# Perceiver block on one core: logits one block sooner, a Sinkhorn chain's lead of 12, and tile 2 mixed by TensorE

## What is computed

```
x_norm = x * rsqrt(mean(x * x) + eps)
H_res_logits = (x_norm @ W_res.T).reshape(B, T, 4, 4) + H_res_base     # pre and post likewise, 4 each
step, 50 times:  u = -logsumexp(Z + v, axis=-1);  v = -logsumexp(Z + u, axis=-2)      # Z = logits / 0.1
H_res = exp(Z + u + v);  H_res = (1 - g) * I + g * H_res
x_pre = einsum('btnc,btn->btc', x_streams, softmax(H_pre_logits));  y = x_pre @ W_branch
out = x + einsum('btij,btjc->btic', H_res, x_streams) + einsum('btc,btn->btnc', y, softmax(H_post_logits))
```

## Time and profile before

| | |
|---|---|
| median of 3 runs | 1117.78 us (1116.27, 1117.78, 1118.06) |
| the profiled execution | 1117.16 us |
| its span | 1115.4 us |
| granted TensorE clock, mean | 0.986 |
| busy: TensorE, VectorE, ScalarE, GpSimd | 95%, 73%, 43%, 17% |
| chain that ended last, by engine | TensorE 88%, VectorE 9%, DMA 1%, ScalarE 1% |

### The profile page before, as it was taken

The page is one execution under the profiler, slowest core; times in us unless marked ns, Lnnn a source line. Parts: engine busy times, 40 slices in busy tenths (PEclk is TensorE's granted clock), DMA queues, the critical chain, the costliest instruction groups (busy, mean ns, idle before and its releaser), DMA issues.

```text
span 1115.4 us, 17534 instructions
## 1 busy us (share of the span) xinstructions
PE 1057.4 (95%) x6308; PEld 888.9 (80%) x6308; DVE 816.2 (73%) x1862; ACT 475.9 (43%) x1012; POOL 190.6 (17%) x186
## 2 busy tenths in 40 slices
PE   5999999999999999999999999999999999998727
PEld 3888888788888888888888888888888878886515
DVE  6787667676667879766668877666627788837998
ACT  4553444344444446544444465423213344432315
POOL 0000000233223232333233220000001032320000
PEclk9999999999999999999999999999999999999878
DMA  9785676245543333344445312799935423000001
GB/s 240 150 204 127 153 163 156 50 109 109 113 98 86 75 76 72 70 94 97 112 95 108 76 38 52 161 217 241 210 68 104 73 42 57 3 14 1 1 1 76
DMA packets 184540, 111.26 MB, mean 100 GB/s; under 512 B 108040, under 2 KB 174344, under 8 KB 184480
## 3 DMA queue, kind: packets, MB, share of 16 engines
q1 hardware_dynamic: 182224, 109.37, 45.4%
q10 hardware_dynamic: 2256, 1.11, 0.4%
HBM read 90.98 MB, written 18.94 MB: 99 GB/s over the span
## 4 chain that ended last, share of the span: by engine, by line
PE 88%; DVE 9%; DMA 1%; ACT 1%; issue 0%; ACTq 0%; POOL 0%; DVEq 0%
PE ps L606 32%; PE ps L513 15%; PE ps L573 14%; PE ps L941 9%; PE ps L499 4%; PE ps L634 4%; PE ps L617 4%; PE ps L717 1%; DVE small L2051 1%; DVE small L2055 1%; DVE small L2043 1%; DVE small L2047 1%; DVE small L2039 1%; DVE small L2035 1%; DVE xr L2185 1%; DMA raw<-in_L_xattn_q_proj_w 1%
## 5 line engine op out<-in xcount | busy, mean ns | idle before, releaser
L606 PE MATMUL ps<-wt,act 128*128 128x512 f32 x1536 | 381.0, 394 | 0.0
L606 PEld LDWEIGHTS ps<-wt,act 128*128 128x128 f32 x1536 | 278.1, 188 | 51.8 <-issue 0.4
L513 PE MATMUL ps<-wt,act 128*128 128x512 f32 x768 | 178.0, 393 | 3.9 <-DVE wt L1507 3.9
L513 PEld LDWEIGHTS ps<-wt,act 128*128 128x128 f32 x768 | 145.2, 190 | 34.6 <-DVE act L1491 4.3
L573 PE MATMUL ps<-act,wt 128*128 128x512 f32 x672 | 153.7, 390 | 0.0
L1062 ACT ACTIVATE wt<-raw 128x512 fp32r<-128x512 f32 x192 | 106.3, 625 | 94.4 <-PE ps L513 52.3
L573 PEld LDWEIGHTS ps<-act,wt 128*128 128x128 f32 x672 | 125.9, 188 | 26.0
L1499 DVE STREAM_TRANSPOSE raw<-raw 128x1024 f32<-128x1024 f32 x92 | 107.9, 1217 | 22.1 <-DMA raw<-in_L_xattn_o_proj_w 22.1
L1507 DVE TENSOR_TENSOR wt<-raw,wt 128x512 fp32r<-128x512 f32 x176 | 110.0, 683 | 17.3 <-ACT wt L1062 17.2
L941 PE MATMUL ps<-wt,act 128*128 128x512 f32 x480 | 121.3, 400 | 0.0
L2202 POOL TENSOR_TENSOR small<-small 128x4 f32<-128x4 f32 (+2 forms) x64 | 68.9, 1079 | 257.0 <-DVE small L1521 211.5
(11 more groups left out here) (162 smaller groups left out, 1226.9 us busy)
## 6 DMA issues: line engine op xcount, KB each, us to landing
xr<-in_ctx SPq DMA_DIRECT2D x64, 256.0 KB, 4.8
raw<-in_L_xattn_o_proj_w SPq DMA_DIRECT2D x32, 512.0 KB, 14.3
raw<-in_L_xattn_q_proj_w SPq DMA_DIRECT2D x28, 512.0 KB, 9.1
xr<-q_rows SPq DMA_DIRECT2D x16, 512.0 KB, 4.2
ot_hi<-spare SPq DMA_DIRECT2D x64, 128.0 KB, 2.0
act<-ot_hi SPq DMA_DIRECT2D x32, 256.0 KB, 9.6
q_rows<-G SPq DMA_DIRECT2D x28, 256.0 KB, 2.6
raw<-in_L_xattn_k_proj_w SPq DMA_DIRECT2D x8, 512.0 KB, 7.1
```

Of the source, the lines that this page charges most:

```text
L513: mm = pe.matmul(banks[t], lhs(p == 2, c, t), wt[:, n_slot, int(p == 1), c, :], start=(acc_from and q == 0), stop=(acc_to and q == 3 * NC ...
L606: mm = pe.matmul(bank, src[int(p == 2)][:, c, kt * P:(kt + 1) * P], wt[:, slot, int(p == 1), c, :], start=(q == 0), stop=(q == 3 * NC - 1))
```

## The change

It does five things. (1) The transposes and logits of tiles 0 and 1 stand earlier among TensorE's matmuls: logits of tile 0 in block 11 in place of block 12, logits of tile 1 after six matmuls of block 12 in place of after it. ScalarE's `normalise_out(0)` stands ahead of the copies for tile 1. (2) VectorE starts chain 0 ahead of the add of block 12, and runs 12 of its iterations alone, not 8. (3) TensorE mixes both halves of tile 2. Its second half goes into bank 0, which tile 0 had; an added matmul by the identity first puts `xr` into it. VectorE mixes (3, 0) and (3, 1) side by side, and no more. (4) TensorE waits ahead of tile 1's mixing until chain 1 has done all but 42 of its steps (seven iterations). (5) The store of (2, 1) stands last in SyncE's list.

The diff (`CHAIN_STEPS` is 304, the steps of a chain up to the end of its last iteration):

```diff
@@ -36,7 +36,8 @@
 ROW = 4
 NSTR, CW = 4, 256
 ITERS, EPOCH = 50, 25
-LEAD = (1, 3, 3, 1)
+LEAD = (4, 3, 3, 1, 1)
+CHAIN_STEPS = 8 + 6 * (ITERS - 1) + 2
 LAST = ((0, 0), (1, 0), (0, 1), (1, 1), (2, 0), (3, 0), (2, 1), (3, 1))
 TURNED = {(0, 0): (1, 0), (0, 1): (2, 0), (1, 0): (3, 1), (1, 1): (4, 2),
           (2, 0): (5, 3), (3, 0): (6, 5), (2, 1): (7, 4), (3, 1): (8, 7)}
@@ -160,6 +161,7 @@
         lg = [ps[:, 2, 0:24], ps[:, 4, 0:24]]
         open_banks = [(ps[:, 0, :], ps[:, 1, :]), (ps[:, 2, :], ps[:, 3, :]), (ps[:, 4, :],), (ps[:, 5, :],)]
         late_base = ps[:, 6:8, 256:512]
+        mix_banks = open_banks[0:2] + [(ps[:, 4, :], ps[:, 0, :])]
         kacc = [ps[:, 2, :], ps[:, 3, :]]
         vacc = [ps[:, 6, :], ps[:, 7, :]]
         sacc = ps[:, 4, :]
@@ -481,7 +483,7 @@
             for a, n, w in ((0, 16, w_res), (16, 4, w_pre), (20, 4, w_post)):
                 sp.dma_start(w24[a:a + n, :], w).then_inc(w24_loaded, 16)
             for t, half, signal, count in ((0, None, mix_out, 2), (1, None, mix_out, 4), (2, 0, mix_out, 5),
-                                           (2, 1, out_ready, 1), (3, 0, out_ready, 2), (3, 1, out_ready, 3)):
+                                           (3, 0, out_ready, 1), (3, 1, out_ready, 2), (2, 1, mix_out, 6)):
                 sp.wait_ge(signal, count)
                 part = slice(0, E) if half is None else slice(half * UW, (half + 1) * UW)
                 sp.dma_start(out_rows[:, t, part], xr[:, t, part]).then_inc(out_stored, 16)
@@ -922,11 +924,11 @@
 
             def mix(t):
 
-                ready = 16 * t if t < 2 else 32 + 8 * (t - 2)
-                for half, bank in enumerate(open_banks[t]):
+                for half in range(2):
+                    bank = mix_banks[t][half]
                     for i in (2 * half, 2 * half + 1):
                         for j in range(NSTR):
-                            pe.wait_ge(d_res, ready + 4 * i + j + 1)
+                            pe.wait_ge(d_res, 16 * t + 4 * i + j + 1)
                             mm = pe.matmul(bank[:, (i % 2) * CW:(i % 2 + 1) * CW], dres[t % 2][:, 4 * i + j, :],
                                            z[:, t, j * CW:(j + 1) * CW], start=False, stop=(i % 2 == 1 and j == NSTR - 1))
                     mm.then_inc(mix_done, 1)
@@ -972,6 +974,8 @@
                 def at_5():
                     if 3 <= b <= 10:
                         weigh2(b - 3)
+                    if b == 12:
+                        logits(1)
 
                 def at_11():
                     if b == 0:
@@ -979,10 +983,6 @@
                     elif b == 11:
                         turn_rows(0, 0)
                         turn_rows(0, 1)
-                    elif b == 12:
-                        logits(0)
-                        turn_rows(1, 0)
-                        turn_rows(1, 1)
                     elif b == 13:
                         turn_rows(2, 0)
                     elif b == 14:
@@ -995,6 +995,9 @@
                         turn_out2(b - 3)
                     if 1 <= b <= 8:
                         turn_query(b - 1)
+                    if b == 11:
+                        turn_rows(1, 0)
+                        logits(0)
                     if b == 15:
                         logits(2)
                         logits(3, 0, 4)
@@ -1017,15 +1020,18 @@
                     for c in range(NC):
                         mm = pe.matmul(ps[:, 3, 192:216], ones, w24T[:, c, :], start=(c == 0), stop=(c == NC - 1))
                     mm.then_inc(s24_done, 1)
-                if b == 12:
-                    logits(1)
+                    turn_rows(1, 1)
             turn_rows(3, 1)
             logits(3, 4, NC)
             for t in range(NT):
                 branch(t)
                 base(t)
-            for t in range(3):
-                mix(t)
+            mix(0)
+            pe.wait_ge(sk_step[1], CHAIN_STEPS - 42)
+            mix(1)
+            pe.wait_ge(mix_out, 1)
+            pe.matmul(mix_banks[2][1], ident[:], xr[:, 2, UW:E], start=True, stop=False)
+            mix(2)
 
 
         def ctx_dst(dst, p, kt):
@@ -1425,11 +1431,11 @@
 
             copy_rows(0, 0)
             copy_rows(0, 1)
+            normalise_out(0)
+            copy_rows(1, 0)
             sc.wait_ge(s24_done, 1)
             sc.activation(s24, ps[:, 3, 192:216], ACT.Copy).then_inc(s24_ready, 1)
-            copy_rows(1, 0)
             copy_rows(1, 1)
-            normalise_out(0)
             normalise_out(1)
             exp_chain(0)
             copy_rows(2, 0)
@@ -1449,23 +1455,23 @@
                 sc.wait_ge(h_ready, t // 2 + 1)
                 if t >= 2:
                     sc.wait_ge(mix_done, 2 * (t - 2) + 2)
-                for n in range(16 if t < 2 else 8):
+                for n in range(16):
                     sc.activation(dres[t % 2][:, n, :], ident[:], ACT.Copy, scale=hres[:, 16 * t + n:16 * t + n + 1]
                                   ).then_inc(d_res, 1)
 
             def mixed(t, half):
-                k = 2 * t + half if t < 2 else 2 + t
-                sc.wait_ge(mix_done, k + 1)
-                sc.activation(xr[:, t, half * UW:(half + 1) * UW], open_banks[t][half], ACT.Copy).then_inc(mix_out, 1)
+                sc.wait_ge(mix_done, 2 * t + half + 1)
+                sc.activation(xr[:, t, half * UW:(half + 1) * UW], mix_banks[t][half], ACT.Copy).then_inc(mix_out, 1)
 
             diagonals(0)
             diagonals(1)
             mixed(0, 0)
             mixed(0, 1)
             mixed(1, 0)
+            mixed(1, 1)
             diagonals(2)
-            mixed(1, 1)
             mixed(2, 0)
+            mixed(2, 1)
 
 
         @block.vector
@@ -2122,11 +2128,11 @@
 
             add_last(1, 1)
             logits(0)
-            add_last(2, 0)
             logits(1)
             centre_rows(0)
             centre_cols(0)
             first_iteration3(0)
+            add_last(2, 0)
             for _ in range(LEAD[0]):
                 iterate((0,))
             add_last(3, 0)
@@ -2136,8 +2142,10 @@
             for _ in range(LEAD[2]):
                 iterate((0,))
             logits(2)
+            for _ in range(LEAD[3]):
+                iterate((0,))
             add_last(3, 1)
-            for _ in range(LEAD[3]):
+            for _ in range(LEAD[4]):
                 iterate((0,))
             logits(3)
             centre_rows(1)
@@ -2187,8 +2195,7 @@
                                  out_ready if (i % 2, j) == (1, NSTR - 1) else dv)
 
             v.wait_ge(base_added, 3)
-            mix(((2, 1), (3, 0)))
-            mix(((3, 1),))
+            mix(((3, 0), (3, 1)))
 
 
         @block.gpsimd
```

## The result

| | before | changed |
|---|---|---|
| median of 20 runs | 1117.74 us | 1114.82 us |
| lowest to highest | 1116.17 to 1120.19 | 1113.61 to 1118.19 |
| the profiled execution | 1117.16 | 1116.33 |
| its span | 1115.4 | 1114.5 |

The ratio is 0.9976 (95% interval 0.9969 to 0.9982): 2.7 us faster, between 2.0 and 3.5. The medians differ by 2.9 us. Forecast were 1114.6 us, a gain of 2.9.

What follows compares the result with a forecast made beforehand. Bound: second chain's start, 50 iterations, VectorE's mixing and a store. Gains of 2.3 us (work, issue) and 0.6 (landing) make 2.9: 1114.3 from the profiled execution, 1114.9 from the median, forecast 1114.6 us; range 1113.0 to 1116.4.

Steps and rivals of the forecast that it cites:

- What bounds the kernel: End of kernel: set by the second chain's start, its 50 iterations of 1.39 us, VectorE's 24 mixing pieces and a store.
- Point 1: TensorE, blocks 11 to 12: second logits end 4.2 us sooner, at 999.9; the new order costs nothing.
- Point 2: VectorE around the last adds: twelve iterations fit with 0.2 us to spare; first chain's result comes 5.55 us sooner.
- Point 3: Mixing: starts sooner on ScalarE and TensorE, the timed wait costs 0, ScalarE's last copy ends at 1109.9.
- Point 4: VectorE's final mixing: 16 pieces, not 24, end at 1108.4; 3.7 us less, of which ScalarE leaves 2.2.
- Point 5: Last stores: the last finds the queue empty and lands in 2.1 us, not 2.7; 0.6 us gain.
- The sum: End of kernel: 2.3 us from work and issue plus 0.6 us from landing, together 2.9 us.
- rival B: VectorE before the last block's add: twelve iterations don't fit, second chain 1.4 us late, gain 1.5 us; chance 0.15.
- Rival C in its partial form: Mixing on TensorE: clock comes back 1 us later, 0.5 us of it lands on the end; likelier than full C.
- The full form: TensorE mixes tile 2 at the lower clock, 6.9 us more; kernel 4.0 us slower, about 1121; chance 0.05.

Runs made afterwards that it cites:

- front_only: Kernel before with only the new logits order and the lead of 12 iterations, old mixing kept: 1115.98 us, ratio 0.9992.
- tail_only: Changed kernel's new mixing and store order, with the kernel before's logits order, VectorE adds and lead of 8: 1120.91 us, ratio 1.0031.
- before_stores: Kernel before with SyncE's store of (2, 0) moved behind those of (2, 1) and (3, 0): 1117.32 us, ratio 0.9992.
- warm: Changed kernel plus seven unused 256-column products before tile 0, wait ahead of tile 1 at 33 steps, not 42: 1113.72 us, ratio 0.9971.
- narrow_more: Changed kernel with tile 2's eight 24-column logits products made twice in block 15, first time for nothing: 1118.25 us.

## Why the prediction was right, point by point

- *What bounds the kernel.* Right, and the two halves of the change show it: the end was VectorE's 24 pieces (`front_only` left them and gained nothing but the stores' part), and what ScalarE and TensorE do ahead of chain 1's result is free only while it fits (`tail_only`).
- *Point 1, the order at nothing.* Right. In the changed kernel the second logits end at 999.8 (999.9 forecast), with no idle time of TensorE in blocks 11 to 14.
- *Point 2, twelve iterations fit.* Right, with 0.56 us to spare (0.2 worked out) where the clock didn't fall, and chain 1 starts 5.4 us behind the last six matmuls with eight iterations or with twelve. Chain 0's result stands 5.5 us further ahead.
- *Point 3, ScalarE and TensorE.* Tiles 0 and 1: 16.2 us (16.1). First matmul of tile 2: 0.84 us behind the result (0.7). Last copy ended 8.65 us behind it (8.4). The wait cost nothing, as worked out.
- *Point 4.* 16 pieces in 6.80 us; VectorE ended 1.85 us ahead of ScalarE.
- *Point 5, the stores.* Landing 2.0 us (2.1), and `before_stores` shows the crowding by itself. Here the row of the trace was followed and not the figure of the Trainium skill, and the row was right.
- *The sum.* 2.8 us in the tail of the two traces, 2.7 (2.0 to 3.5) in the times, 2.9 forecast. The terms behind it are a little off and cancel: the end of the work gained 1.9 us (2.2 forecast), the issue and the landing 0.8 (0.7 forecast), and 0.1 lies behind the landing. In the other traces that mix tile 2 by TensorE with the lead and a cold start, the tail is 10.7 to 11.5 us, a gain of 2.3 to 3.2 over the one trace of before. That the medians agree with the forecast this closely is in part luck.
- *What the median also holds.* Among executions with a clock above 0.983, the median of the changed kernel is 1114.44 (15 executions), that of the kernel before 1116.71 (36, beside the groups): 2.3 us. Among the others it is 1116.53 (5) against 1118.14 (44): 1.6 us. The medians of all differ by more, since the changed kernel had fewer falls, 5 of 20 against 44 of 80. Whether the change does that or chance did is open; nothing in the prediction asks for it.
- *Slips in the working.* The sum gives 1114.3 from the profiled execution and 1114.9 from the median; the forecast of 1114.6 is the middle, and the metric is the median. The range doesn't follow from its own terms: 1116.3 less 3.5 and 1118.1 less 1.3 are 1112.8 and 1116.8, not 1113.0 and 1116.4. The clock came back 4.1 us after the mixing began, not 3.9. None of this moves the result out of the range.
- *What was missing.* The text named a late start of chain 1 as the sign of rival B. The sign came, and B was not the cause: the last adds waited for TensorE at the half clock. A sign that only says "late" doesn't tell who was late; the idle time before the add does (1.58 us; under B there would be none). The fall stood in no term, no rival and no range, though both kernels have it; the one trace of before happened not to show it. It widened the times (4.6 us from lowest to highest) more than the change moved them.
- *Rival C in its partial form* is real: the clock did not come back at the same moment after the mixing began, and tiles 0 and 1 took from 15.5 to 16.7 us in the eight traces with the new mixing or the new lead and no warm start. Before, VectorE's longer part hid that; now up to 0.8 us of it reaches the end, and `warm` takes it out. The full form, tile 2 at the half clock, never came.

## What to carry to other kernels

Work taken from the engine that ends last is worth only what the engine that takes it over has free at that moment: here 8 pieces moved alone cost 3.5 us, the same move behind an earlier start gained 2.7. Look also at what the last transfer has in front of it in the queue: four stores at once cost the last one 0.7 us. And where one profiled execution disagrees with the median, compare stretches that begin at the same event in both (here: chain 1's result to the end), before you explain the difference by the change.

## What was not expected of the hardware

TensorE's clock fell from 2.4 to 1.2 GHz while the engine was busy without a gap: in the changed kernel's trace at 1023.2, 0.2 us after twelve products of 24 columns had ended, in `before_stores` at 1024.2, 0.7 us after the same twelve, in `narrow_more` at 1024.8, 0.3 us after twenty. It cost 1.8 to 2.3 us. It came in a quarter of the executions with twelve such products by the times, in nearly half by the clock (69 of 151), in 6 to 9 of 11 with twenty, and in none or one of 19 with at most four together. The Trainium skill's "TensorE: Matmul & The Clock Gate", in "Why this matters for your kernels", tells of falls by idle gaps longer than those here. The traces agree in that gaps of 0.8 us left the clock up in `warm`; but it also fell with no gap at all, after narrow work.
